# Products with the states in attention: from tiles of 64x128 to tiles of 64x64

## What is computed

```python
def step(carry, qkv):                       # for each token, batch and head
    S_K, C_QV, G = carry                    # 64 x 64 each
    q_t, k_t, v_t = qkv
    k_C = jnp.einsum('bhk,bhkv->bhv', k_t, C_QV)
    G = G + k_t[..., :, None] * k_C[..., None, :]
    S_K = S_K + k_t[..., :, None] * k_t[..., None, :]
    C_QV = C_QV + q_t[..., :, None] * v_t[..., None, :]
    S_C = jnp.einsum('bhkj,bhjv->bhkv', S_K, C_QV)
    o_t = jnp.einsum('bhk,bhkv->bhv', q_t, S_C - G)
    return ((S_K, C_QV, G), o_t)
```

## Time and profile before

| | |
|---|---|
| median of 3 runs | 1142.39 us (1141.29 to 1143.08) |
| the profiled execution | 1139.75 us, span 1138.0 us |
| TensorE busy | 1082.0 us, 95% of the span |
| VectorE, ScalarE, GpSimd busy | 688.9, 573.2, 211.3 us |
| the attention stage | about 284.6 to 972 us |

### The profile page before, as it was taken

The page is one execution under the profiler, slowest core; times in us unless marked ns, Lnnn a source line. Parts: engine busy times, 40 slices in busy tenths (PEclk is TensorE's granted clock), DMA queues, the critical chain, the costliest instruction groups (busy, mean ns, idle before and its releaser), DMA issues.

```text
span 1138.0 us, 26569 instructions
## 1 busy us (share of the span) xinstructions
PE 1082.0 (95%) x11150; PEld 968.4 (85%) x11150; DVE 688.9 (61%) x1281; ACT 573.2 (50%) x1001; POOL 211.3 (19%) x177
## 2 busy tenths in 40 slices
PE   5897799998999999999999999999999999879998
PEld 4675588897899989899989889988899989868897
DVE  6999797881444574355465445466446447567773
ACT  4222666662555454545454554545545454636663
POOL 2326362120010101001010010011000110131230
PEclk8999999999999999999999999999999999989999
DMA  9100361002543524543552453444353354101101
GB/s 298 30 1 1 119 209 44 0 1 74 186 137 123 180 85 131 169 148 109 171 168 76 167 176 105 149 158 126 117 180 110 113 167 150 38 1 38 35 22 56
DMA packets 96418, 124.23 MB, mean 109 GB/s; under 512 B 8880, under 2 KB 86576, under 8 KB 95536
## 3 DMA queue, kind: packets, MB, share of 16 engines
q1 hardware_dynamic: 96304, 122.59, 34.0%
HBM read 79.57 MB, written 42.99 MB: 108 GB/s over the span
## 4 chain that ended last, share of the span: by engine, by line
PE 69%; DVE 5%; ACT 1%; issue 1%; DMA 0%; SPq 0%; POOL 0%; DVEq 0%; ACTq 0%; POOLq 0%
PE bank L1091 10%; PE bank L201 5%; PE bank L1111 5%; PE bank L202 5%; PE bank L203 5%; PE bank L1103 5%; PE bank L1145 4%; PE bank L1193 3%; PE bank L1194 3%; PE bank L1177 3%; PE bank L1133 2%; PE bank L1128 2%; PE bank L1161 2%; PE bank L1162 2%; PE bank L1160 2%; PE bank L1178 2%
## 5 line engine op out<-in xcount | busy, mean ns | idle before, releaser
L1026 POOL TENSOR_TENSOR ot_lo<-o_sum,ot_hi 128x512 fp32r<-128x512 f32 x64 | 82.6, 1291 | 628.4 <-ACT ot_hi L1325 626.0
L1374 ACT COPY ut<-bank 64x512 f32<-64x512 f32 x128 | 74.3, 580 | 139.4 <-PE bank L1111 137.0
L1430 DVE TENSOR_TENSOR sc_a<-bank,causal 128x512 f32<-128x512 f32 x128 | 79.4, 682 | 102.0 <-PE bank L1091 96.5
L201 PE MATMUL bank<-ln_xhi,ring_hi 128*128 128x512 f32 x256 | 102.5, 400 | 3.8 <-POOL state L1014 3.3
L202 PE MATMUL bank<-ln_xlo,ring_hi 128*128 128x512 f32 x256 | 100.6, 393 | 0.0
L203 PE MATMUL bank<-ln_xhi,ring_lo 128*128 128x512 f32 x256 | 100.4, 392 | 0.0
L1430 DVE TENSOR_TENSOR ln_xn<-bank,causal 128x512 f32<-128x512 f32 x128 | 79.4, 682 | 30.7 <-PE bank L1091 30.7
L1441 DVE STREAM_TRANSPOSE k<-kt 128x512 f32<-128x512 f32 x64 | 43.3, 696 | 72.9 <-ACT kt L1315 72.9
L1315 ACT COPY qt<-bank 128x512 f32<-128x512 f32 x64 | 37.5, 588 | 75.3 <-PE bank L203 75.3
L1378 ACT COPY o_sum<-bank 64x512 f32<-64x512 f32 x128 | 74.2, 580 | 2.4
L1517 DVE TENSOR_TENSOR xres<-bank,xres 128x512 f32<-128x512 f32 x32 | 22.0, 687 | 87.2 <-PE bank L1162 87.0
(11 more groups left out here) (139 smaller groups left out, 2982.7 us busy)
## 6 DMA issues: line engine op xcount, KB each, us to landing
k_rows_scratch<-k SPq DMA_DIRECT2D x32, 512.0 KB, 2.9
k<-k_rows_scratch SPq DMA_DIRECT2D x128, 128.0 KB, 3.0
ring_hi<-wqk_hi_scratch SPq DMA_DIRECT2D x60, 256.0 KB, 4.4
ring_lo<-wqk_lo_scratch SPq DMA_DIRECT2D x60, 256.0 KB, 5.7
u_rows_scratch<-sc_a SPq DMA_DIRECT2D x30, 512.0 KB, 2.6
sc_a<-u_rows_scratch SPq DMA_DIRECT2D x120, 128.0 KB, 3.1
out_dram<-xres SPq DMA_DIRECT2D x16, 256.0 KB, 2.1
xres<-in_L_attn_a_x_dram SPq DMA_DIRECT2D x4, 512.0 KB, 7.2
```

What stands on the lines that cost most here:

```text
L201: nc.tensor.matmul(out, w_hi, x_hi, start=(k == 0), stop=False)
L1026: nc.gpsimd.tensor_tensor(ot_lo[:, g, :, :].rearrange("p m t -> p (m t)"), o_sum[:, (j - 1) % 2, g, :], ot_hi[:, g, :, :].rearrange("p m t ...
L1374: nc.scalar.copy(ut[half(h), g, :, :].rearrange("p m t -> p (m t)"), bank[CB[x]][half(h), :])\
L1430: nc.vector.tensor_tensor(to[:, x, :, :], bank[SB[x]][:, :].rearrange("p (m t) -> p m t", m=4), causal[:, None, :].to_broadcast([P, 4, P]) ...
```

## The change

Each matmul of by_state is split in four. The 128 tokens are taken in two groups r of 64, and the 128 columns of the state in two halves x. A matmul then has 64 rows, 64 weight columns and 64 streamed columns, and its output lies on the partitions `half(x)`. The order within an (g, m) is r, then h, then x, so that four matmuls in a row use the four quarters of the array.

```diff
                             p, b = hf * GP + g * 2 + m // 2, m % 2
-                            for h in range(2):
-                                nc.tensor.matmul(bank[CB[2 * g + h]][:, m * P:(m + 1) * P], state[half(h), hf, g, m, :],
-                                                 qt[half(h), p, b, c, :], start=(m == 0), stop=False, skip_group_check=True)
+                            for r in range(2):
+                                tok = slice(r * DK, (r + 1) * DK)
+                                for h in range(2):
+                                    for x in range(2):
+                                        nc.tensor.matmul(bank[CB[2 * g + h]][half(x), m * P + r * DK:m * P + (r + 1) * DK],
+                                                         state[half(h), hf, g, m, half(x)], qt[half(h), p, b, c, tok],
+                                                         start=(m + r == 0), stop=False, skip_group_check=True)
```

## The result

The changed kernel took 1185.32 us (median of 4 runs, 1183.79 to 1188.36); the kernel before, in runs beside it, 1141.84 us. The ratio is 1.038, with a 95% interval of 1.036 to 1.041: 43 us slower. The forecast was 1154.7, so the direction was right and the size was not: 12 us more were forecast and 43 measured.

What follows compares the result with a forecast made beforehand. TensorE, busy 95% of the span, was taken as the bound. Array +2.6, changes of form +11.0 and absorbed waiting -1.3 gave +12.3 us: 1152.0 on the profile's scale, 1154.7 on that of the runs, range 1146 to 1213.

Steps and rivals of the forecast that it cites:

- The array's own time: by_state on TensorE: four tiles a round take 1.87 us a unit in place of 1.78, +2.6 us over 32 units.
- Change of tiling: Into and out of by_state's 64x64 tiles: 0.15 us going in and 0.20 going back, 11.0 us in all.
- What hides it: Three long ut blocks after by_state: their waiting for other engines absorbs 0.43 us each, -1.3 us; 2.1 at most.
- Feeding four tiles: Weight load and matmul pairs in by_state: at 0.018 us a pair, 25 queued ahead, feeding takes 1.85 us, within the array's 1.87.
- fed too slowly in part: Rival, by_state: 0.018 us a pair with nothing queued ahead gives +26 us, 1168; at 0.022, +42, 1184; chance 0.20.
- One pair per 0.029 us: Rival, by_state: four tiles run no faster than two, 3.72 us a unit, +71 us, 1213; chance 0.26 for 0.024 to 0.029.
- No drain: Rival, around by_state: changing only the column split costs nothing, +2.6 - 0.2 remain, 1144.8; chance 0.07.
- faster: Rival, by_state: four tiles share away a round's fixed part, 1.70 us a unit, -2.7 us, 1139.7 without a drain; chance 0.04.

## Why the prediction was wrong

**The array's own time: right.** "If four tiles run in a round" they take 32 rounds of 0.058, 1.87 us. Measured from start to start: 2.03, of which 0.16 belong to the change of form.

**Change of tiling: right.** Forecast 0.35 us a unit. In the unit shown the three blocks grew from 1.89, 1.78 and 1.89 to 1.98, 2.03 and 1.98, +0.43 in all, of which the forecast gave 0.08 to the array and 0.35 to the forms. Over 32 units this is 13.8 us; forecast 13.6 before absorption. The kernels without reloads measure the two steps alone: 15.3 us. The runs show the price of the change of form, and not what the engine does in it. The edit that splits only the tokens keeps the form and has the kt scores at their old length.

**What hides it: small as forecast, and read one step too short.** I had put the three long blocks down to waiting for other engines. That is what the trace shows, VectorE's masks behind ScalarE's rows of u, but what makes those late are the reloads, as both are gone without them. The blocks can give 2.1 us at most, so nothing hangs on it.

**Feeding four tiles: the step that failed.** The step asked at what pace the engine takes its instructions, and found 0.018 us a pair just enough. It was: in every by_state without a stop, four tiles ran at the array's pace, 2.03 / 128 = 0.016 us a pair with the change of form in it. What it did not ask is where the instructions come from. The page of before had the row for it, TensorE's program as 86 packets of 16 KB on q8, and the sum put it at nothing without a word. The missing term: 21.1 us of idle at the borders of the pieces, and about 6 us from the lower clock behind three of the stops, where the forecast had the clock at 1.00 throughout. The latter is worked out from the stretches at 0.50, some 5.5, 3.4 and 3.4 us of work after 376.1, 668.3 and 1006.2 us, in which about half is loss, 6.2. 13.8 + 21.1 + 6 = 41 of the 44.0 us. The remaining 3 are in the main a matter of counting: from start to start the 14 stops take 24.6 us, since the modelled end of the last matmul covers the beginning of each. On the other side stand up to 2.1 us of the three long blocks of before.

**The rivals.** The range up to 1213 holds the measured time, but only since it was drawn wide for an engine fed too slowly. The measured time lies where "fed too slowly in part" with 0.022 us a pair had it (1184), but its mechanism did not occur: that asked for by_state at 2.3 to 2.6 us in every unit, and the units that stop nowhere have 2.03. One pair per 0.029 us is refuted by the same number. "No drain" and "faster" fall with the 15.3 us that the kernels without reloads differ by. The Trainium skill's floor of about 25 ns from start to start (TensorE: Matmul & The Clock Gate, Back-to-back issue gap) does not hold across tiles here: 128 starts in 2.02 us are 15.8 ns each. The Trainium skill's rule of the drain (TensorEngine Tiling, Tiling Modes) agrees with the 0.35 us a unit: a change of only the column split is not free.

The Trainium skill also has a rule on the term that was missed, and I did not weigh it. Runtime: NRT & Kernel Launch, Instruction fetch mechanics, says that the program is fetched in blocks of 16 KB, 256 instructions, one ahead, and that crossing a border is mostly hidden, because instructions are issued more slowly than they are fetched. The trace agrees with the block and not with the conclusion: 256 instructions of by_state are used in 2.02 us, from border to border it can be 2.3, and while the DMA engines were full none came in 7.2 us.

## What to carry to other kernels

Count the instructions as well as the work: where an edit trades few large matmuls for many small ones, work out in how many microseconds a 16 KB piece of the program is used (here 2.0; at before's 64 instructions in 1.79 it was 7), and look whether data transfers fill the DMA engines in the same stretch. A stop marked "issue" in lines that the edit does not touch is the sign of it. Neither alone did harm here: the change's instructions without the reloads gave no stop, nor did the reloads with before's instructions. And here two row tiles of a full-width product already filled the array (32 rounds of 0.058 us do the work of 16 of 0.111), so four quarters could win nothing and paid for each change of form.

## What was not expected of the hardware

- Pieces of the program come late behind data: none came in the 7.2 us before 569.2, at a mean DMA share of 0.78, and TensorE stood still for up to 4.1 us elsewhere. When each piece was asked for, the rows don't tell, nor what holds it up: that it stands behind the data's packets is the likely reading. What they do tell is that TensorE passed no border earlier than 1.2 us behind the landing of its piece.
- An idle of 4.07 us took the granted clock from 1.00 to 0.50, and it stayed there for about 5.5 us of dense work; stops of 2.3 us (668.3) and 2.0 us (1006.2) had the same effect for 3.4 us each, but one of 3.2 us (888.2) had none, nor had that of 1.5 us at 570.0. The length of the idle alone does not decide it.
- The granted clock fell to 0.50 in a stretch in which TensorE had no idle at all by its records (matmuls of 32 columns behind loads of 128), and the run cost +300 us in place of the +168 forecast.
